# Moving the conversion of four weight tiles out of the ramp, and re-ordering loads, stores and scalings of a fused attention and FFN kernel on eight cores

## The chip, the cores and the metric

The kernel runs on all eight NeuronCores of one Trainium2 chip. Each core gets two of the sixteen batch entries and does the whole layer for them, with no traffic between cores. The metric is the device time in microseconds of the slowest core.

## The reference

```python
h = layernorm(x)                                  # x: 16 x 2048 x 1024 float32
q, k, v = h @ Mq, h @ Mk, h @ Mv                  # 8 heads, 64 wide for q and k, 128 for v
scores = einsum('bhqk,bhck->bhqc', q, k)          # q, k, v are plain reshapes to (b, h, 2048, .)
att = softmax(scores / 8, axis=1)                 # over the query axis, of each (b, h)
x = x + layernorm(att @ v)
wg, wu, wd = (w_int * (1 / 127) for w_int in (w_gate, w_up, w_down))   # int32 weights, 3072 hidden
f = (silu(h2 @ wg.T) * (h2 @ wu.T)) @ wd.T        # h2 = layernorm(x)
x = x + layernorm(f)
```

The reshape to heads takes rows of the sequence into a head: a head's 2048 positions are 256 rows of x. The softmax runs over queries, so its sums belong to the rows of V, which are scaled by their reciprocals before the second product.

## The kernel before, in words

**The ramp and the projection.** A core holds 32 tiles of 128 rows of x, in eight blocks of four tiles. `load_x(T)` loads tile T into one of four buffers `xl`, `ln1(T)` normalises it to bf16 `xn` (statistics on VectorE, the power -0.5 on GpSimd, the scaling on ScalarE, whose `finish` also issues the load of tile T+4), and `turn(T)` transposes it on TensorE into `xnT` (L282, copied out by ScalarE, for T = 2 and 3 by VectorE). `proj_units(blk, ...)` makes sixteen units of eight matmuls 128x128x512 of a block: four for q, four for k, eight for v (L327). `evac` empties their banks, VectorE and ScalarE by turns. Blocks 0 to 3 use four PSUM banks (`wide`), blocks 4 to 7 two, because the attention has started beside them. The results go to scratch in HBM: `qk_d` from `qst` and `kst`, `v_d` from `vst`, with stores on SP's queue. The float32 weights mq, mk and mv come as three loads that cast to bf16, on GpSimd's queue.

**The attention.** It is cut into 256 steps K. A step's score unit `s_unit(K)` makes four matmuls into S, one ScalarE instruction makes the exponentials with their sums (L432), `v_scale(K, c)` multiplies the left (c = 0) and the right (c = 1) half of the V tile by the reciprocal sums on VectorE (L440, L441), and `av_unit(K, c)` makes 16 matmuls 128x128x128 into banks O. A V tile's halves lie in twelve buffers `vt`: slots 0 to 5 for c = 0, 6 to 11 for c = 1. `av_unit(K, c)` issues the load of step K+6 into the slot that it has just read (`load_v`, on SP's queue). `unload` adds O to `y2`, and after sixteen steps `half_stats` and `ln2` normalise, add x (tiles that `load_x1` has loaded a second time, into `x1`) and build the bf16 `x2T` for the FFN.

**The FFN.** Eight blocks n of 512 rows. For each of 24 hidden tiles `gate_unit` and `up_unit` make eight matmuls each from `wgu` (four buffers, bf16, gate and up of one hidden tile) and `x2T`; then sixteen `down_unit` make twelve each from `hT` and `wd`. The gate and up weights are int32 in HBM, 1 MB a hidden tile. `convert(c)` is a DMA on GpSimd's queue from HBM to HBM that casts two hidden tiles to bf16 scratch `gu_bf`; twelve of them stand at fixed units of the projection (L716, L717), each behind a wait for the matmul before it. `load_wgu(i)` loads a 0.5 MB tile from that scratch, 192 times, on SP's queue; `load_wd` casts the down weights in FFN block 0.

**What sets the order.** The program is written out by a planner on the host. Every engine executes its own list, in the order in which the planner emitted it, and each DMA stands in the list of the engine that issues it (`P.dma("sync", ...)`, `"gpsimd"`, `"scalar"`). `P.tick` and `P.spent` move the planner's clock by the units' estimated times; `P.later(d, fn)` emits fn once that clock is d us further. `run_side` puts score and AV units between the main units. Per four steps the side order is: AV of steps 4Q and 4Q+1, c = 0, behind the score unit of 4Q+3; AV of 4Q+2 and 4Q+3, c = 0, behind 4Q+4; c = 1 of the first two behind 4Q+5, of the last two behind 4Q+6. The attention runs 41 steps beside blocks 4 to 7 of the projection, and 32 beside each FFN block. An engine that waits for one instruction holds all that stand behind it in its list.

## Time and profile before

| | us |
|---|---|
| median of three runs (1749.59 to 1753.48) | 1753.07 |
| profiled execution, its device time | 1755.92 |
| its span (first to last instruction, slowest core, core 1) | 1754.4 |
| spans of the eight cores | 1731.6 to 1754.4 |
| TensorE busy in the span | 1669.3 |
| VectorE, ScalarE, GpSimd busy | 951.2, 814.8, 125.5 |
| granted TensorE clock of core 1, mean | 0.983 |

Busy times are of core 1, the slowest. In the rows of the trace PE is TensorE, DVE is VectorE, ACT is ScalarE, POOL is GpSimd, SPq is SyncE's instruction queue; L76 is the helper that issues every DMA and L72 the one that issues every matmul, so such rows are told apart by tile names. A name such as `F<-wv,xnT` gives what is written and what is read, with buffer numbers left out.

### The profile page before, as it was taken

The page shows a single profiled execution, that of the slowest core. Times are in us where ns is not written, and L with a number is a line of the kernel's source. Part 1 is how long each engine was busy: PE and PEld are TensorE (multiplying, and loading weights), DVE is VectorE, ACT ScalarE, POOL GpSimd, SP SyncE. Part 2 cuts the span into 40 slices and gives each one's busy share as a digit, 9 for nine tenths or more (in the row PEclk, how much of TensorE's full clock was granted, in tenths as well). Part 3 has the DMA queues.
Part 4 walks back from the last instruction along what each step waited for, and adds up shares of the span by engine and source line. Part 5 has one row for each costly group of instructions (what it writes and reads, how often), then busy time and mean ns, then how long its engine had stood idle before and what let it go on. Part 6 is the DMA issues. An engine that isn't in the chain of part 4 may idle for free.

```text
span 1754.4 us, 32046 instructions; the slowest of 8 cores (1731.6 to 1754.4 us)
## 1 busy us (share of the span) xinstructions
PE 1669.3 (95%) x11008; PEld 795.4 (45%) x11008; DVE 951.2 (54%) x2123; ACT 814.8 (46%) x984; POOL 125.5 (7%) x257
## 2 busy tenths in 40 slices
PE   5999888879999999999999999999999999999998
PEld 2444444434444444444444444444444444444443
DVE  3433446355646565656465656575657565655433
ACT  3444556445535454455445545454455444542111
POOL 2111001000101000100010001000100010001000
PEclk9999999989999999999999999999999999999999
DMA  9899997978982656265626563666256625651531
GB/s 191 175 190 216 201 170 143 196 152 215 235 213 85 205 168 178 88 202 160 186 88 193 168 189 85 185 171 195 88 169 180 198 78 171 167 160 52 157 96 48
DMA packets 212446, 281.02 MB, mean 160 GB/s; under 512 B 48320, under 2 KB 132288, under 8 KB 212288
## 3 DMA queue, kind: packets, MB, share of 16 engines
q1 hardware_dynamic: 199568, 255.91, 51.5%
q0 software_dynamic: 12720, 23.07, 10.4%
q8 instruction: 91, 1.49, 0.4%
q14 instruction: 67, 0.55, 0.1%
HBM read 260.05 MB, written 46.14 MB: 175 GB/s over the span
## 4 chain that ended last, share of the span: by engine, by line
PE 76%; DMA 8%; DVE 7%; ACT 4%; issue 3%; SPq 1%; POOL 1%; DVEq 0%; ACTq 0%; POOLq 0%
PE F L72 55%; PE O L72 13%; PE S L72 7%; DMA vt<-v_d 5%; ACT E L432 1%; DMA xl<-x 1%; DMA wgu<-gu_bf 1%; ACT y L500 1%; DMA wq<-mq 1%; SPq L76 1%; DVE x L507 1%; DVE hT L573 1%; DVE bnB L487 0%; ACT y L251 0%; DVE y L470 0%
## 5 line engine op out<-in xcount | busy, mean ns | idle before, releaser
L72 PE MATMUL F<-x2T,wgu 128*128 128x512 bf16 x3072 | 764.5, 380 | 14.5 <-DVE rsx L440 3.9
L432 ACT ACTIVATE E<-S 128x2048 bf16<-128x2048 f32 x256 | 480.4, 1876 | 542.1 <-PE S L72 542.1
L72 PEld LDWEIGHTS F<-x2T,wgu 128*128 128x128 bf16 x3072 | 260.1, 97 | 359.4 <-issue 157.6
L72 PE MATMUL F<-wd_sb,hT 128*128 128x512 bf16 x1536 | 357.6, 379 | 0.4 <-ACT y L601 0.4
L72 PEld LDWEIGHTS O<-vt,E 128*128 128x128 bf16 x4096 | 271.0, 98 | 147.8 <-issue 37.4
L72 PE MATMUL O<-vt,E 128*128 128x128 bf16 x4096 | 313.4, 220 | 21.0 <-DVE vt L441 19.4
L550 DVE SCALAR_TENSOR_TENSOR th<-th,F 128x512 f32<-128x512 f32 x192 | 131.8, 687 | 347.9 <-ACT th L546 347.8
L441 DVE TENSOR_SCALAR vt<-vt,rsx 128x512 bf16<-128x512 bf16 x512 | 179.3, 351 | 94.8 <-DMA vt<-v_d 49.4
L72 PEld LDWEIGHTS F<-wd_sb,hT 128*128 128x128 bf16 x1536 | 141.6, 98 | 168.2 <-issue 23.6
L72 PE MATMUL S<-qk 64*128 64x512 bf16 x1024 | 158.1, 388 | 5.6 <-ACT E L432 5.3
L546 ACT ACTIVATE th<-F 128x512 f32<-128x512 f32 x192 | 113.4, 591 | 72.8 <-PE F L72 72.7
L573 DVE TENSOR_TENSOR hT<-th,F 128x512 bf16<-128x512 f32 x192 | 131.1, 683 | 19.7 <-DVE vt L441 10.2
L470 DVE TENSOR_TENSOR y<-y,O 128x512 f32<-128x512 f32 x192 | 122.8, 680 | 25.1 <-PE O L72 25.0
L72 PE MATMUL F<-wv,xnT 128*128 128x512 bf16 x384 | 95.8, 387 | 3.2 <-ACT kst L314 2.2
L72 PEld LDWEIGHTS S<-qk 64*128 64x128 bf16 x1024 | 29.5, 94 | 117.3 <-issue 117.3
L500 ACT ACTIVATE y<-y,nbB,rsB 128x512 f32<-128x512 f32 x64 | 48.6, 806 | 65.2 <-POOL nbB L247 65.2
L237 POOL TENSOR_TENSOR rsB<-vfB,mhalf 128x1 f32<-128x1 f32 x64 | 39.2, 612 | 512.5 <-DVE vfB L235 469.8
L613 POOL TENSOR_TENSOR rsC<-vfC,mhalf 128x1 f32<-128x1 f32 x31 | 20.5, 662 | 715.0 <-DVE vfC L611 715.0
L255 DVE TENSOR_TENSOR x<-x,y 128x1024 f32<-128x1024 f32 x31 | 38.0, 1224 | 58.8 <-ACT y L251 58.8
L251 ACT ACTIVATE y<-y,nbC,rsC 128x1024 f32<-128x1024 f32 x31 | 38.3, 1236 | 51.6 <-POOL nbC L247 51.6
L72 PE MATMUL F<-xnT,wk 128*128 128x512 bf16 x192 | 51.5, 409 | 10.5 <-DVE rsx L440 10.0
L251 ACT ACTIVATE xn<-xl,nbA,rsA 128x1024 bf16<-128x1024 f32 x32 | 39.7, 1240 | 44.4 <-POOL nbA L247 44.3
(75 smaller groups left out, 886.2 us busy)
## 6 DMA issues: line engine op xcount, KB each, us to landing
wgu<-gu_bf SPq DMA_DIRECT2D x192, 512.0 KB, 4.8
vt<-v_d SPq DMA_DIRECT2D x512, 128.0 KB, 3.0
xl<-x SPq DMA_DIRECT2D x32, 512.0 KB, 10.5
x<-x SPq DMA_DIRECT2D x32, 512.0 KB, 6.2
out<-x SPq DMA_DIRECT2D x31, 512.0 KB, 3.2
gu_bf<-gu POOLq DMA_DIRECT2D x12, 1024.0 KB, 18.7
v_d<-vst SPq DMA_DIRECT2D x16, 512.0 KB, 14.6
qk<-qk_d SPq DMA_DIRECT2D x16, 512.0 KB, 5.8
```

What stands on the lines that cost most here:

```text
L72: "tensor", lambda t: t.matmul(out, lhsT, rhs, start=start, stop=stop),
L237: return P.pool(lambda g: g.tensor_tensor(rs[:, s:s + 1], vf[:, s:s + 1], mhalf[:, 0:1], AL.pow), t, const_done)
L251: return P.act(lambda a: a.activation(dst[:, :], y[:, :], AF.Identity, bias=nb[:, s:s + 1], scale=rs[:, s:s + 1]), *waits)
L255: return P.dve(lambda v: v.tensor_tensor(xt[:, :], xt[:, :], y[:, :], AL.add), *waits)
L432: lambda s: s.activation(to, S[:, :], AF.Exp, scale=0.125, accum_out=accx[:, K % 16:K % 16 + 1]),
L441: vs_tok[K, c] = P.dve(lambda v: v.tensor_scalar(v_[:, :], v_[:, :], r, None, AL.mult), rs_tok[K], v_tok[K, c])
L470: t = P.dve(lambda v, d=d, part=part: v.tensor_tensor(part, part, O[d][:, :], AL.add), done, y2_tok[u, d])
L500: t = [P.act(lambda e, part=part: e.activation(part, part, AF.Identity, bias=nbB[:, s:s + 1], scale=rsB[:, s:s + 1]), shift) for part in h ...
L546: tanh = P.act(lambda s: s.activation(t_[:, :], F[0][:, :], AF.Tanh, scale=1.0 / 254.0), done, th_read[i - 1] if i else None, *(() if i el ...
L550: bank_free["F0"] = gated[i] = P.dve(lambda v: v.scalar_tensor_tensor(t_[:, :], t_[:, :], 1.0, F[0][:, :], AL.add, AL.mult), tanh)
L573: lambda v: v.tensor_tensor(dst, t_[:, :], F[1][:, :], AL.mult), done, gated[i],
L613: b = P.pool(lambda g: g.tensor_tensor(rsC[:, s:s + 1], vfC[:, s:s + 1], mhalf[:, 0:1], AL.pow), b, const_done)
```

## The change

It does these things, in the order of the program:

- Tiles 0 to 3 of x are loaded straight into `x1` and kept there; `load_x1` skips them. Tiles 4 to 7 are loaded once the first half of mk has landed. Loads of tiles 8 to 31 are issued by ScalarE.
- mk and mv come in two pieces each, mk's by rows and mv's by columns, and the two of mk are issued between the first normalisations. A one-element activation stands at the start of ScalarE's list.
- Block 0's four key units become `keys_at_once`, which goes through four banks at each of eight row slices and waits for mk's second piece at the fifth. Block 1's q and k units become sixteen `narrow_unit` of 256 columns, so that the first eight need only tiles 4 and 5. V units of blocks 0 and 1 come left halves first.
- Stores of q and k are issued by ScalarE, 1.4 us later by the planner's clock. V is stored for two blocks at once, in pieces of 512 elements in place of 256, by ScalarE for pairs 0 and 2 and by SyncE for pairs 1 and 3; `load_v` waits for the one store that it needs.
- `v_scale` is emitted later: 9.0, 9.0, 6.5, 3.6 us (c = 0) and 20.0, 15.5, 14.0, 11.0 us (c = 1) behind the step's exponential by K % 4, in place of 3.6 and 6.5; `av_unit` emits it if it has not been.
- Twenty hidden tiles are converted, one by one, ten of them from unit 22 in steps of four and ten from the tenth unit of block 4 in steps of five. Hidden tiles 0 to 3 are cast straight into `wgu` by GpSimd's queue in FFN blocks 0 and 1, and in block 1 `keep_wgu` stores them to the scratch, from which the other six blocks load them.
- `load_wgu` is emitted 1.7 us later, the down weights come in 24 loads of one tile from unit 3 on, and the second `half_stats` hangs on a place in the side order.

```diff
-SLOT = 5.1
+CAST = 4
...
     def load_x(T, *waits):
-        xl_tok[T] = P.dma("sync", xl[T % 4][:, :],
-                          x_hbm[T // 16, 128 * (T % 16):128 * (T % 16 + 1), :],
-                          q_xl[T % 4], *waits)
+        dst, q = (x1[T], q_x1[T]) if T < 4 else (xl[T % 4], q_xl[T % 4])
+        xl_tok[T] = P.dma("sync" if T < 8 else "scalar", dst[:, :],
+                          x_hbm[T // 16, 128 * (T % 16):128 * (T % 16 + 1), :], q, *waits)
+        if T < 4:
+            x1_tok[T] = xl_tok[T]
...
-        ready = ln_stats(xl[s], bnA, mvA, vfA, rsA, s, EPS, xl_tok[T])
+        src = x1[T] if T < 4 else xl[s]
+        ready = ln_stats(src, bnA, mvA, vfA, rsA, s, EPS, xl_tok[T])
...
-                load_x(T + 4, t, w_tok[0])
+            t = xl_free[T] = xn_tok[T] = ln_scale(xn[s], src, rsA, nbA, s, ready, busy)
+            if 8 <= T + 4 < 32:
+                load_x(T + 4, t)
...
-        if T in (2, 3) or T >= 20 and T % 2:
+        if T in (0, 1, 2, 3, 4, 6) or T >= 20 and T % 2:
...
+        def keys_at_once():
...
+            for dt in range(8):
+                for i, (name, ap) in enumerate(four):
+                    first = [bank_free.get(name), *ready, *w_ready[1][:1]] if dt == 0 else \
+                        w_ready[1][1:] if dt == 4 else ()
+                    tok = P.mm(ap, wk[:, 512 * dt + 128 * i:512 * dt + 128 * (i + 1)],
+                               xT[:, 512 * dt:512 * (dt + 1)], dt == 0, dt == 7, first, done=dt == 7)
+                    done.append(tok)
...
+        def narrow_unit(which, i, g):
...
+            for dt in range(8):
+                first = [bank_free.get(name), *w_ready[which],
+                         *(xnT_tok[4 * blk + 2 * g + j] for j in range(2))] if dt == 0 else ()
+                done = P.mm(ap[:, 0:256], w[:, 512 * dt + 128 * i:512 * dt + 128 * (i + 1)],
+                            xT[:, 512 * dt + 256 * g:512 * dt + 256 * (g + 1)], dt == 0, dt == 7, first,
+                            done=dt == 7)
+            P.spent(4 * MM, 0.5)
...
+        def qk_store(which, ev=None):
...
-                    "sync", bass.AP(qk_d.tensor, row, [[2048, 128], [128 * 2048, 2], [1, 1024]]),
+                    "scalar", bass.AP(qk_d.tensor, row, [[2048, 128], [128 * 2048, 2], [1, 1024]]),
...
+            P.later(1.4, store)
...
-            ready = [w_tok[2], xnT_tok[4 * blk + j]]
+            ready = [w_tok[f"v{c2}"], xnT_tok[4 * blk + j]]
...
+            st = vst[2 * (pair % 2) + half]
+            dst = bass.AP(st, 2048 * c2 + 256 * par + 128 * hh, [[4096, 128], [512, 4], [1, 128]])
+            v_ev[blk, j, c2] = bank_free[name] = evac(dst, ap, done, v_stored.get((pair - 2, half)))
+            if par and hh == 1 and c2 == 1:
...
+                def store():
+                    v_stored[pair, half] = P.dma(
+                        "scalar" if pair % 2 == 0 else "sync",
+                        bass.AP(v_d.tensor, (16 * b + half) * 131072 + 512 * (pair % 2),
+                                [[1024, 128], [2 * 131072, 8], [1, 512]]),
+                        bass.AP(st, 0, [[4096, 128], [512, 8], [1, 512]]), q_vs[2 * (pair % 2) + half], *ev)
+                if pair % 2:
+                    store()
+                else:
+                    P.later(1.4, store)
...
+        if blk == 0:
+            units[4:8] = [keys_at_once]
+        if blk == 1:
+            units[0:8] = [lambda w=w, i=i, g=g: narrow_unit(w, i, g)
+                          for g in range(2) for w in range(2) for i in range(4)]
...
-        stored = [v_stored[4 * b + 2 + p, h] for p in range(2) for h in range(2)]
         v_tok[K, c] = P.dma("sync", vt[i][:, :], v_d[16 * b + t, :, 512 * c:512 * (c + 1)], q_v[i],
-                            *stored, av_tok[K - 6, c] if K >= 6 else None)
+                            v_stored[2 * b + c, t % 2], av_tok[K - 6, c] if K >= 6 else None)
...
     def load_x1(n):
+        if n < 4:
+            return
...
-        P.later(3.6, lambda: v_scale(K, 0))
-        P.later(6.5, lambda: v_scale(K, 1))
+        P.later((9.0, 9.0, 6.5, 3.6)[K % 4], lambda: v_scale(K, 0))
+        P.later((20.0, 15.5, 14.0, 11.0)[K % 4], lambda: v_scale(K, 1))
...
     def v_scale(K, c):
+        if (K, c) in vs_tok:
+            return
...
     def av_unit(K, c):
+        v_scale(K, c)
...
-            for d in range(2):
-                P.later(1.5 + SLOT * d, lambda d=d: half_stats(G, c, d))
+            P.later(1.5, lambda: half_stats(G, c, 0))
+            if G == 1:
+                P.later(4.1, lambda: half_stats(G, c, 1))
+            else:
+                hooks[side_at[0] + 4] = lambda: P.later(1.5, lambda: half_stats(G, c, 1))
...
-        ht = i % NHT
-        wgu_tok[i] = P.dma("sync", bass.AP(wgu[i % 4], 0, [[2048, 128], [1024, 2], [1, 1024]]),
-                           gu_bf[ht, :, :, 0:1024], q_wgu[i % 4],
-                           conv_tok[ht], *([wgu_read[i - 4]] if i >= 4 else xl_idle))
+        ht, free = i % NHT, [wgu_read[i - 4], conv_tok[(i - 4) % NHT]] if i >= 4 else xl_idle
+        if i < 2 * NHT and ht < CAST:
+            wgu_tok[i] = P.dma("gpsimd", wgu[i % 4][:, :], gu_hbm[ht, :, :], q_cast[i % 4], *free)
+        else:
+            wgu_tok[i] = P.dma("sync", bass.AP(wgu[i % 4], 0, [[2048, 128], [1024, 2], [1, 1024]]),
+                               gu_bf[ht, :, :, 0:1024], q_wgu[i % 4], conv_tok[ht], *free)
+    def keep_wgu(ht):
+        conv_tok[ht] = P.dma("sync", gu_bf[ht, :, :, 0:1024],
+                             bass.AP(wgu[ht % 4], 0, [[2048, 128], [1024, 2], [1, 1024]]), q_keep[ht],
+                             wgu_tok[NHT + ht])
...
+        if n == 1 and ht < CAST:
+            keep_wgu(ht)
...
-            load_wgu(i + 4)
+            P.later(1.7, lambda: load_wgu(i + 4))
...
+            if side_at[0] in hooks:
+                hooks.pop(side_at[0])()
...
+    load_w("q", 0, wq, mq_hbm, 512, (0, 8), (0, 512), xl_tok[0])
+    ln1(0)
+    load_w("k0", 1, wk, mk_hbm, 512, (0, 4), (0, 512))
+    P.tick(1.75)
+    ln1(1)
+    load_w("k1", 2, wk, mk_hbm, 512, (4, 4), (0, 512))
+    for T in range(4, 8):
+        load_x(T, w_tok["k0"])
+    P.tick(1.75)
+    w_ready = [[w_tok["q"]], [w_tok["k0"], w_tok["k1"]]]
+    ln1(2)
+    turn(0)
...
     def convert(c, *waits):
-        conv_tok[2 * c] = conv_tok[2 * c + 1] = P.dma(
-            "gpsimd", bass.AP(gu_bf.tensor, 2 * c * 256 * ROW, [[2 * ROW, 256], [ROW, 2], [1, 1024]]),
-            bass.AP(gu_hbm.tensor, 2 * c * 262144, [[2048, 256], [1024, 2], [1, 1024]]), q_conv[c], *waits)
+        conv_tok[c] = P.dma(
+            "gpsimd", bass.AP(gu_bf.tensor, c * 256 * ROW, [[2 * ROW, 128], [ROW, 2], [1, 1024]]),
+            bass.AP(gu_hbm.tensor, c * 262144, [[2048, 128], [1024, 2], [1, 1024]]), q_conv[c], *waits)
...
-    first = u0[0:8] + u1[0:8] + u0[8:16] + u1[8:16]
+    for unit in u0[0:4]:
+        unit()
+        P.tick(4 * MM)
+    ln1(4)
+    ln1(5)
+    load_w("v0", 3, wv, mv_hbm, 1024, (0, 8), (0, 512))
+    u0[4]()
+    turn(4)
+    turn(5)
+    ln1(6)
+    ln1(7)
+    load_w("v1", 4, wv, mv_hbm, 1024, (0, 8), (512, 512))
+    for unit in u1[0:8]:
+        unit()
+    turn(6)
+    turn(7)
+    for unit in u1[8:16]:
+        unit()
+    first = u0[5::2] + u0[6::2] + u1[16::2] + u1[17::2]
...
-    early_conv = {22: 0, 32: 1, 42: 2, 52: 3}
-    later_conv = {(4, 6): 4, (4, 14): 5, (5, 6): 6, (5, 14): 7, (6, 6): 8, (6, 14): 9, (7, 4): 10, (7, 10): 11}
...
+    early_conv = {22 + 4 * c: CAST + c for c in range(10)}
+    later_conv = {(4 + u // 16, u % 16): CAST + 10 + c for c, u in enumerate(range(9, 59, 5))}
...
-            if blk == 7 and u == 4:
+            if blk == 7 and u in (3, 6, 9, 12):
                 xl_idle = [*(xl_free[T] for T in range(28, 32)), xn_read[28]]
-                for i in range(4):
-                    load_wgu(i)
+                load_wgu(u // 3 - 1)
...
     def load_wd(c, *waits):
-        src = bass.AP(wd_hbm.tensor, 2 * c * 131072, [[1024, 128], [131072, 2], [1, 1024]])
-        dst = bass.AP(wd, 2 * c * 1024, [[NHT * 1024, 128], [1024, 2], [1, 1024]])
-        wd_tok[:] = [P.dma("gpsimd", dst, src, q_wd, *ramp_idle, *waits)]
-    first_block = {}
-    for c in range(12):
-        first_block[6 + 4 * c // 3] = lambda *w, c=c: load_wd(c, *w)
+        wd_tok[:] = [P.dma("gpsimd", wd[:, 1024 * c:1024 * (c + 1)], wd_hbm[c, :, :], q_wd,
+                           *ramp_idle, *waits)]
...
-            if n == 0 and ht in first_block:
-                first_block[ht](("c_tensor", P.count["c_tensor"]))
+                if n == 0 and 3 <= 2 * ht + (unit is up_unit) <= 41:
+                    at = 2 * ht + (unit is up_unit) - 3
+                    for c in range(24 * at // 39, 24 * (at + 1) // 39):
+                        load_wd(c, ("c_tensor", P.count["c_tensor"]))
```

**Where the order changes.** VectorE's list in FFN block 1, around the scaling of the V tiles of steps 96 to 98 (vt0 to vt2 are their left halves, vt6 and vt7 the right halves of 96 and 97; bnB, bnC, y2, y4 and x1 belong to the normalisations). Before:

```order
L440 RECIPROCAL rsx<-accx 128x1
L441 TENSOR_SCALAR vt0<-vt0,rsx 128x512
L487 BN_STATS bnB<-y2_1 128x6
L441 TENSOR_SCALAR vt6<-vt6,rsx 128x512
L440 RECIPROCAL rsx<-accx 128x1
L441 TENSOR_SCALAR vt1<-vt1,rsx 128x512
L487 BN_STATS bnB<-y2_1 128x6
L608 BN_STATS bnC<-y4_0 128x6
L441 TENSOR_SCALAR vt7<-vt7,rsx 128x512
L440 RECIPROCAL rsx<-accx 128x1
L441 TENSOR_SCALAR vt2<-vt2,rsx 128x512
```

In the change the same stretch of VectorE's list, a piece of eight rows left out:

```order
L508 RECIPROCAL rsx<-accx 128x1
L509 TENSOR_SCALAR vt0<-vt0,rsx 128x512
L559 BN_STATS bnB<-y2_1 128x6
L692 BN_STATS bnC<-y4_0 128x6
L508 RECIPROCAL rsx<-accx 128x1
L509 TENSOR_SCALAR vt1<-vt1,rsx 128x512
...
L508 RECIPROCAL rsx<-accx 128x1
L509 TENSOR_SCALAR vt2<-vt2,rsx 128x512
L509 TENSOR_SCALAR vt6<-vt6,rsx 128x512
L509 TENSOR_SCALAR vt7<-vt7,rsx 128x512
```

The right halves (vt6, vt7) moved from right behind their left halves to behind step 98's left half.

GpSimd's list at the start. Before, the loads of mk and mv stand behind the four normalisations of block 0:

```order
L76 DMA wq<-mq 128x8x512
L237 TENSOR_TENSOR rsA<-vfA,mhalf 128x1
L247 TENSOR_SCALAR nbA<-mvA,rsA 128x1
...
L76 DMA wk<-mk 128x8x512
L76 DMA wv<-mv 128x8x1024
```

In the change:

```order
L76 DMA wq<-mq 128x8x512
L244 TENSOR_TENSOR rsA<-vfA,mhalf 128x1
L254 TENSOR_SCALAR nbA<-mvA,rsA 128x1
L76 DMA wk<-mk 128x4x512
L244 TENSOR_TENSOR rsA<-vfA,mhalf 128x1
L254 TENSOR_SCALAR nbA<-mvA,rsA 128x1
L76 DMA wk<-mk 128x4x512
...
L76 DMA wv<-mv 128x8x512
```

The first half of mk moved up past three normalisations, the second past two.

SyncE's list from the end of the first four projection blocks. Before, stores of q, k and v and loads of x stand among the V loads:

```order
L76 DMA v_d<-vst 128x8x256 x2
L76 DMA qk<-qk_d 128x2048
L76 DMA qk<-qk_d 64x1024 x2
L76 DMA vt<-v_d 128x512 x12
L76 DMA xl<-x 128x1024 x2
L76 DMA qk_d<-qst 128x2x1024
L76 DMA xl<-x 128x1024
```

In the change:

```order
L76 DMA v_d<-vst 128x8x512 x2
L76 DMA qk<-qk_d 128x2048
L76 DMA qk<-qk_d 64x1024 x2
L76 DMA vt<-v_d 128x512 x12
L76 DMA qk<-qk_d 128x2048
L76 DMA qk<-qk_d 64x1024 x2
L76 DMA vt<-v_d 128x512 x26
```

The loads of x and the stores of q and k have left this list; they now stand in ScalarE's, between its copies.

## Rows read from the trace of the kernel before

**Rows 1.** Core 1 by stretches: length, busy PE, PEld, DVE, ACT, POOL, PEclk, DMA share, GB/s.

```profile
0.00:62.90 62.90, 39.91 (x193) 18.90 (x194) 23.45 (x53) 21.70 (x23) 11.39 (x28) 0.95 0.89 192
62.90:160.00 97.10, 97.10 (x528) 47.09 (x526) 38.32 (x79) 42.70 (x52) 13.52 (x31) 1.00 0.97 186
160.00:200.00 40.00, 35.69 (x264) 17.20 (x262) 16.16 (x43) 26.79 (x31) 3.03 (x7) 1.00 1.05 212
200.00:400.00 200.00, 166.04 (x1199) 81.78 (x1196) 99.12 (x244) 103.87 (x122) 16.92 (x32) 0.89 0.84 170
400.00:560.00 160.00, 153.62 (x1056) 73.34 (x1054) 93.80 (x212) 77.80 (x96) 17.60 (x30) 0.99 0.79 194
560.00:737.70 177.70, 175.74 (x1218) 84.20 (x1216) 106.05 (x240) 89.30 (x109) 9.86 (x20) 1.00 0.54 158
```

**Rows 2.** Timeline of the ramp: start us, us, engine line op [idle before <-releaser].

```profile
13.13 0.69 DVE L229 BATCH_NORM_STATS2 bnA<-xl 128x6 f32<-128x512 f32 x1
...
18.50 1.93 PE L292 MATMUL tp<-ident,xn 128*128 128x128 bf16 x16 [4.31 <-ACT xnT L300]
...
21.37 3.57 PE L72 MATMUL O<-xnT,wq 128*128 128x512 bf16 x8 [0.94 <-DVE xnT L298]
...
34.33 3.27 PE L72 MATMUL O<-xnT,wk 128*128 128x512 bf16 x8 [3.17 <-DMA wk<-mk]
...
47.29 3.50 PE L72 MATMUL O<-xnT,wq 128*128 128x512 bf16 x8 [1.25 <-ACT xnT L300]
...
62.79 1.89 PE L72 MATMUL O<-wv,xnT 128*128 128x512 bf16 x8
64.51 1.67 PE L72 MATMUL F<-wv,xnT 128*128 128x512 bf16 x7
```

**Rows 3.** DMA queues (packets, MB, share of 16 engines) and issues (median us to landing).

```profile
q1 hardware_dynamic: 199568, 255.91, 51.5%
q0 software_dynamic: 12720, 23.07, 10.4%
...
wv<-mv POOLq DMA_DIRECT2D x1, 2048.0 KB, 38.9
```

**Rows 4.** Waits from 160 to 560 us: total, times, longest.

```profile
DVE vt L441 <- DMA vt<-v_d: 49.4, 13, 10.9
...
PE O L72 <- DVE vt L441: 19.4, 5, 8.8
...
PE F L72 <- DVE rsx L440: 10.9, 4, 6.6
```

**Rows 5.** Timeline around 210 us.

```profile
210.60 0.35 DVE L441 TENSOR_SCALAR vt<-vt,rsx 128x512 bf16<-128x512 bf16 x1 [5.97 <-DMA vt<-v_d]
...
214.74 0.68 DVE L313 CAST kst<-F 128x512 bf16<-128x512 f32 x1
...
215.56 1.87 PE L72 MATMUL F<-xnT,wk 128*128 128x512 bf16 x4 [6.63 <-DVE rsx L440]
```

**Rows 6.** The chain of waits from 160 to 520 us: start us, us, what.

```profile
189.27 21.24 DMA vt<-v_d
...
231.98 15.06 DMA vt<-v_d
...
312.10 15.81 DMA vt<-v_d
...
334.96 19.33 DMA vt<-v_d
...
486.07 18.53 DMA wgu<-gu_bf
```

**Rows 7.** SyncE's queue from 90 to 137 us.

```profile
102.06 8.85 SPq L76 DMA_DIRECT2D xl<-x  x1
...
134.73 9.99 SPq L76 DMA_DIRECT2D qk_d<-qst  x1
```

**Rows 8.** Waits from 560 to 1600 us.

```profile
PE F L72 <- DVE rsx L440: 3.5, 12, 0.4
```

More of the change, by code:

```diff
@@ L145, in build @@
     q_xl = [P.sem(f"q_xl{i}") for i in range(4)]
[L146 removed]
+    q_w = [P.sem(f"q_w{i}") for i in range(5)]
     q_qks = [P.sem(f"q_qks{i}") for i in range(NBLK)]
@@ L350, in qk_unit @@
             if i == 3:
-                ev = [qk_ev[n] for n in range(4)]
-                row = 2 * blk * 128 * 2048 + 1024 * which
+                qk_store(which)
+        def keys_at_once():
+            ready = [xnT_tok[4 * blk + j] for j in range(4)]
+            four, done = [next_bank(banks) for i in range(4)], []
+            for dt in range(8):
[6 more added lines that the diff above has]
+                P.spent(4 * MM, 0.5)
+            for i, (name, ap) in enumerate(four):
+                dst = bass.AP(kst[par], 256 * i, [[2048, 128], [1024, 2], [1, 256]])
+                qk_ev[i] = bank_free[name] = evac(dst, ap, done[28 + i])
+            qk_store(1)
@@ new lines, in narrow_unit @@
+        def narrow_unit(which, i, g):
+            w, st = (wq, qst[par]) if which == 0 else (wk, kst[par])
+            name, ap = next_bank(banks)
+            for dt in range(8):
[4 more added lines that the diff above has]
+                            done=dt == 7)
+            P.spent(4 * MM, 0.5)
+            qk_ev[g, i] = bank_free[name] = evac(
+                st[:, 1024 * g + 256 * i:1024 * g + 256 * (i + 1)], ap[:, 0:256], done)
+            if g and i == 3:
+                qk_store(which, [qk_ev[a, n] for a in range(2) for n in range(4)])
@@ L693, in build, with load_w @@
[L693 to L701 removed]
+    def load_w(name, q, w, src, cols, rows, part, *waits):
+        lo, n = rows
+        at, width = part
+        w_tok[name] = P.dma(
+            "gpsimd", bass.AP(w, lo * cols + at, [[8 * cols, 128], [cols, n], [1, width]]),
+            bass.AP(src.tensor, 128 * lo * cols + at, [[cols, 128], [128 * cols, n], [1, width]]),
+            q_w[q], *waits)
```

73 lines of the change are left out of this document (32 added, 41 removed).

## The prediction

> **What bounds the kernel now.** I read the busy times by stretches first. The reader is to see three regimes of TensorE [rows 1]. In the ramp (0 to 62.9 us) it is busy 39.9 us. In the first four projection blocks (62.9 to 160) it is never idle, though the DMA share is 0.97. From 160 to 400 us it is idle 4.3 + 34.0 = 38.3 us, and its clock is granted at 0.89 of full from 200 on, which with the two levels 2.4 and 1.2 GHz means up to 22% of these 200 us at the lower one and up to 22 us lost by it (less, since some of it falls on idle time). From 400 to 560 it is idle 6.4 us, and from then on it is as good as full: 2.0 us idle in 177.7, where no wait for a V load is listed any more and TensorE's for VectorE's reciprocals are 3.5 us in a thousand [rows 1, 8]. So of 1754 us only the first 560 have anything to give, some 23 + 38 + 6 us of idle and the slow clock, and nothing that speeds up VectorE, ScalarE or the transfers later on is worth a microsecond.
>
> Then the waits of that stretch, for who ends it. VectorE waits 49.4 us for V tiles, TensorE 19.4 us for the scaled V tiles and 10.9 us for VectorE's reciprocals [rows 4]. The timeline shows what the last is: the scaling of a V tile stands in VectorE's list, its load has not landed, the copy of a key bank stands behind it, and TensorE, which wants that bank, waits 6.63 us [rows 5]. It is a wait passed on by the order of VectorE's list, not by its load. The chain has four such loads of 15.1 to 21.2 us from issue to landing, and one load of gate and up weights of 18.5 us [rows 6].
>
> **The change part by part.** *The ramp.* Queries of block 0 start at 21.37, keys at 34.33 after a wait of 3.17 for mk, block 1 at 47.29 and V at 62.79 [rows 2]. Now: the statistics of tile 3 start at 13.13 as before, its transposes no longer wait for ScalarE's copies of tiles 0 and 1 (the 4.31 us), so I put the first query matmul at 19.5, about 1.9 earlier. Queries take 34.33 - 3.17 - 21.37 = 9.8 us as before, clock start included, to 29.3 [rows 2]. The keys need no wait if mk lands by then; it landed at 34.3, and now its halves are issued behind the first and the second normalisation in place of the fourth, and no longer with the whole of mv right behind. 32 matmuls at the pitch of V's (a unit of eight takes 64.51 - 62.79 = 1.72 us [rows 2]) are 6.9 us, to 36.2. Four transposed tiles cost 1.0 each at the slow clock (16 matmuls, 1.93 us [rows 2]); I take 2.4 for the four at full clock. Block 1's eight units' worth of columns is 13.8. That is 52.4. V begins 10.4 us earlier. Ends: 4 us if block 1's tiles or mk come late, since the same 8 MB of float weights must come (mv lands 38.9 us after its issue, rows 3, at 56 us); 12 if nothing waits. I take 10.4, since mv's right half is needed only at 52.4 + 6.9 = 59.3. The warm-up activation costs nothing, it stands where ScalarE is idle.
>
> *Bytes.* Over the whole span the queue of casting transfers took 10.4% of the engines for 23.07 MB, 7.9 us a MB landed; the other 51.5% for 255.91 MB, 3.5 us a MB [rows 3]. A hidden tile is 0.52 MB: 4.1 us to cast, 1.85 to load. Before the FFN the four cast tiles save a load each, 4 x 1.85 = 7.4 us, and the four kept tiles of x 7.4 more: 14.8 us of the DMA's time. The wider pieces of V may save some of the 29 us that its 8.4 MB of stores cost at 3.5 us a MB; I count none of it. In FFN block 1 the casts cost 4 x (4.1 - 1.85) and the stores to scratch 4 x 1.85, 16.4 us of DMA; the DMA share is 0.54 there, 82 us are free, and the tiles are fetched four hidden tiles ahead, some 20 us. It costs nothing. Without that cover it would be a wait for a load like the one of 18.5 us [rows 6], 4 us each beyond what is fetched ahead, 16 in all.
>
> *The projection beside attention.* A right half of step 4Q+6 is loaded behind the AV of step 4Q, one place before its own score unit, and was scaled 6.5 us after that. At the FFN's pace a place is 177.7 / 32 = 5.6 us [rows 1]: 12.1 us of lead. Now it is 5.6 + 14.0 = 19.6. Of the four loads of the chain three are inside 19.6, the fourth is 1.6 us beyond [rows 6]. So of the 19.4 + 10.9 = 30.3 us that TensorE waits for scalings [rows 4] about 80%, 24 us, have their cause removed, and a share of the slow clock with them, some 12 us by the same ratio. Against it: the DMA is busy 1.05 x 40 + 0.84 x 200 = 210 of these 240 us [rows 1], 195 with the bytes saved, and a shorter stretch packs them closer. I take 28 us (20 of idle, 8 of clock), which puts the share at 195 / 212 = 0.92, a share at which the stretch before it runs without a stall [rows 1]. Ends: 8 (only the list's order helps, each late load still ends a wait in TensorE) and 48 (all idle above the later rate, 38.3 - 2.6, and 12 of clock).
>
> *Stores and x loads on ScalarE.* ScalarE is idle for a third to a half of the stretch [rows 1], and an issue on a free queue is short. But SyncE's queue shows issues of 8.9 and 10.0 us in the first four blocks [rows 7], and an issue held that long on ScalarE holds copies. Taken as zero here, a rival below. *FFN block 0:* idle above the later rate is 6.4 - 1.8 = 4.6, and 1.6 of clock; the down weights spread over 98 us in place of 75, so I take 4 (ends 0 and 6). *Everything after:* the scalings of 4Q+1 now stand 9.0 us behind an exponential whose AV follows two places, 10.0 us, later, a margin of 1.0; those of 4Q+3 had 5.0 - 3.6 = 1.4 and gave next to none [rows 8]. Zero, with a rival.
>
> Sum: 10.4 + 28 + 4 = 42.4. The profiled execution took 1755.92, 1.5 more than its span and 2.85 over the median of 1753.07. 1755.9 - 42.4 = 1713.5; against the median 1710.7. I predict 1712.
>
> **The rivals.** *A shared DMA that gives nothing back.* The V loads now share SyncE's list with little else. The rows say only that V loads in a list with stores took 15 to 21 us [rows 6]; whether it waited behind them or beside them they don't say. If beside, landings stay at 15 to 21 us, the earlier start of V packs the same bytes into less time, and the stretch gives 12 in place of 28, the ramp 4: 1755.9 - 4 - 12 - 2 = 1738, 1736 by the median. The Trainium skill, "DMA: Bandwidth & Descriptors", section "Issuing engines are not separate DMA queues", says just this: transfers run on the same 16 engines whoever issues them, and only issue time is saved. Its section "Queues, rings and completion order" says each engine goes round the queues packet by packet, by which a V load would overtake stores of another queue. No run here shows either. Chance 0.18.
>
> *ScalarE held by its own stores.* Two pairs of V stores and the stores around them now stand there. At 9 us each [rows 7], less the 3.4 us that two free banks of 1.72 cover, four are worth some 4 x 5.5 = 22: 1712 + 22 = 1734. Against it speaks that TensorE never idled there [rows 1], so the DMA has room for its work. Chance 0.10.
>
> *Slower: scalings too late.* If the planner's 1.0 us of margin is not there on the chip, the left halves of every fourth step reach TensorE late, in all 64 groups of four. Late by d, that costs 64 x d, and from d = 0.66 us it eats all of the 42. At d = 1 it is 64 us: 1776. The row that speaks against it is the margin of 1.4 us that gave no wait. Chance 0.05.
>
> *More than I take.* All of the middle's 48, 12 in the ramp and 6 in block 0: 1755.9 - 66 = 1690. It needs a DMA share near 1.0 without waits, as from 62.9 to 160. Chance 0.10.
>
> **How the numbers follow.** My forecast, 1700 to 1726, has 0.57. The range takes in the upper part of the better case, all of the held ScalarE and the shared DMA: 1696 to 1740. A measurement of this kernel can tell about 0.2%, 3.5 us. Slower needs the late scalings, or ScalarE's holds together with a shared DMA: 0.05. Within 0.2%: 0.02. Faster: 0.93.
>
> **What would show it.** V's first matmul at 52 us, not 62.8. The row "DVE vt <- DMA" from 160 to 560 down from 49.4 to some 10, and TensorE's waits for scalings from 30 to some 6. Clock of the 200 us before the FFN above 0.94. V loads of 20 us still there, but not in the chain. FFN blocks from the third on 177 us each, as now. Wrong I am if an FFN block takes more than 178.5, if ScalarE shows DMA issues of several us with TensorE waiting behind its copies, or if V starts at 52 and the FFN still starts where it did.

## The result and the profile after

The changed kernel takes 1756.64 us and the kernel before, beside it, 1749.61: medians of 17 executions each, with the three of twenty in which the cores of a die ran at a lower clock left out here and in every median below (with them 1758.78 and 1750.43). The ratio of their times is 1.004, with a 95% interval of 1.0026 to 1.0055: slower by 0.4%, where I had forecast 1712 and had given 0.05 to slower. The profiled execution spans 1755.1 us on core 7, the slowest; the eight cores lie between 1733.4 and 1755.1.

To see where it went I take five moments from the traces, by TensorE's matmuls: the first that reads `wv` (V), the first that writes `S` (scores), the first gate matmul (FFN), and the first gate matmul of FFN block 1, then of block 7. Each is the median of the eight cores, in us from the span's start.

| | V | scores | FFN | block 1 | block 7 | end |
|---|---|---|---|---|---|---|
| before | 62.4 | 161.5 | 371.3 | 554.5 | 1608.2 | 1742.9 |
| after | 54.5 | 167.6 | 364.7 | 552.1 | 1611.8 | 1746.9 |
| the stretch that ends there, after - before | -7.9 | +14.0 | -12.7 | +4.2 | +6.0 | +0.4 |

The last row adds up to +4.0 for the median cores of these two executions; over all runs the slowest core loses some 7 us. These moments are of one execution of each kernel, so the table shows where to look, and the runs below decide. By it two gains came, and three losses that I had priced at nothing, or as a gain, took them back. FFN block 0 (+4.2) is the least certain: taken core by core it lasts 181.0 to 187.6 us before and 180.0 to 193.6 after, medians 184.5 and 187.0.

By stretches, core 7, the columns of [rows 1]:

```profile
0.00:54.50 54.50, 36.68 (x257) 24.13 (x258) 23.09 (x52) 18.45 (x24) 11.80 (x27) 1.00 0.95 199
54.50:171.20 116.70, 98.88 (x532) 47.27 (x531) 43.63 (x91) 46.17 (x55) 19.05 (x42) 0.95 0.97 199
171.20:367.00 195.80, 173.93 (x1331) 87.38 (x1332) 104.25 (x261) 120.62 (x140) 23.35 (x42) 0.98 0.75 155
367.00:560.00 193.00, 176.54 (x1215) 84.29 (x1213) 102.18 (x236) 88.66 (x107) 25.57 (x46) 0.97 0.80 185
711.00:889.90 178.90, 175.40 (x1218) 84.31 (x1216) 104.89 (x241) 89.75 (x109) 11.26 (x20) 1.00 0.53 157
```

The ramp ends 8 us sooner. The first projections, never idle before, are idle 116.7 - 98.9 = 17.8 us, and their clock is 0.95 in place of 1.00. Beside attention the clock is 0.98 on this core and the DMA share is down to 0.75, and TensorE is nevertheless idle 21.9 us. (Over the eight cores, from first scores to FFN, the median clock rose from 0.94 to 0.97, and two cores stayed at 0.94.) FFN block 0 is idle 16.5 us on this core, and a later block takes 178.9 us in place of 177.7.

**Ahead of the first scores.** The chain of waits of core 7:

```profile
96.14 5.20 ACTq L76
...
148.52 11.86 SPq L76
...
162.02 9.07 DMA qk<-qk_d
```

And SyncE's queue in the timeline, which shows what stood ahead:

```profile
144.59 3.83 SPq L76 DMA_DIRECT2D v_d<-vst  x2
148.52 14.07 SPq L76 DMA_DIRECT2D qk<-qk_d  x3
```

The first load of queries and keys is issued behind two V stores of 1 MB each. It is three DMAs: the issue of the first alone takes 11.86 us, the last then lands 9.07 us after its own issue, and TensorE waits. The waits from 160 to 560 us, core 7, answer to [rows 4]:

```profile
PE S L72 <- DMA qk<-qk_d: 13.3, 1, 13.3
...
PE F L72 <- DMA wgu<-gu_bf: 11.7, 2, 9.0
...
PE O L72 <- DVE vt L509: 5.6, 5, 2.0
PE O L72 <- DVE rsx L508: 4.8, 4, 2.2
```

VectorE's waits for V loads, 49.4 us before, have no row any more. Two others stand out: 13.3 us for the first Q/K load, on other cores 4.4 to 14.5, where it was at most 1.1 before, and 11.7 for gate and up tiles, on other cores 0 to 8.2, where it was 2.2 to 7.2 before.

**Beside attention** the rows for `O` are my step in reverse. The timeline of core 0:

```profile
254.93 0.16 DVE L508 RECIPROCAL rsx<-accx 128x1 f32<-128x1 f32 x1
...
255.27 0.35 DVE L509 TENSOR_SCALAR vt<-vt,rsx 128x512 bf16<-128x512 bf16 x1 [0.18 <-DVE rsx L508]
...
255.77 0.70 PE L72 MATMUL O<-vt,E 128*128 128x128 bf16 x8 [2.15 <-DVE rsx L508]
```

No load is late. TensorE has arrived at the AV product, and the scaling is only now made. Nine AV groups on this core wait so (the two rows for `O` read the same here), up to 2.2 us each and 10.4 in all.

**In a later FFN block** (core 7, timeline):

```profile
709.21 0.69 DVE L236 BATCH_NORM_STATS2 bnB<-x 128x6 f32<-128x512 f32 x1
...
709.62 1.52 ACT L572 ACTIVATE y<-y,nbB,rsB 128x512 f32<-128x512 f32 x2 [5.06 <-POOL nbB L254]
...
711.05 1.85 ACT L498 ACTIVATE E<-S 128x2048 bf16<-128x2048 f32 x1
...
713.14 0.61 PE L72 MATMUL S<-qk 64*128 64x512 bf16 x4 [1.71 <-ACT E L498]
```

ScalarE has waited 5.06 us for the norm of one half before it scales `y`; the exponential stands behind that, and TensorE waits 1.71 us for the bank of scores. The waits from 560 to 1600 us put numbers on it, core 7:

```profile
PE S L72 <- ACT E L498: 8.5, 5, 1.7
PE F L72 <- DVE hT L657: 8.3, 6, 1.4
```

Before, core 1, the second had no row of that size (its place was held by [rows 8]), and the first was:

```profile
PE S L72 <- ACT E L432: 4.5, 5, 1.3
```

### The profile page after: what moved, and what is told of

It is laid out like the page before. It is cut to its first block, busy times and chain, and to the rows that moved or that the text cites. A ratio compares the mean times of both kernels' runs of the same rounds, so it can differ in the third digit from the quotient of the medians.

```text
span 1755.1 us, 32318 instructions; the slowest of 8 cores (1733.4 to 1755.1 us)
## 1 busy us (share of the span) xinstructions
PE 1654.7 (94%) x11072; PEld 798.0 (45%) x11072; DVE 945.8 (54%) x2131; ACT 815.7 (46%) x985; POOL 150.8 (9%) x287
## 4 chain that ended last, share of the span: by engine, by line
PE 73%; DVE 9%; DMA 5%; issue 5%; ACT 4%; SPq 1%; ACTq 1%; POOL 1%; DVEq 0%; POOLq 0%
PE F L72 54%; PE O L72 12%; PE S L72 6%; DMA wgu<-gu_bf 2%; ACT E L498 1%; DMA wv<-mv 1%; DVE y L539 1%; DVE x L579 1%; DVE bnB L559 1%; ACT y L572 1%; DVE hT L657 1%; SPq L76 1%; DVE th L634 1%; ACTq L76 1%; DMA wq<-mq 1%
## 5 line engine op out<-in xcount | busy, mean ns | idle before, releaser
L72 PE MATMUL F<-x2T,wgu 128*128 128x512 bf16 x3072 | 763.3, 380 | 28.6 <-DMA wgu<-gu_bf 11.7
L509 DVE TENSOR_SCALAR vt<-vt,rsx 128x512 bf16<-128x512 bf16 x512 | 166.5, 350 | 46.8 <-DVE rsx L508 46.7
L72 PE MATMUL S<-qk 64*128 64x512 bf16 x1024 | 155.9, 383 | 23.5 <-DMA qk<-qk_d 13.3
L244 POOL TENSOR_TENSOR rsB<-vfB,mhalf 128x1 f32<-128x1 f32 x64 | 43.2, 674 | 480.3 <-DVE vfB L242 446.4
L692 DVE BATCH_NORM_STATS2 bnC<-y 128x6 f32<-128x512 f32 x62 | 42.8, 691 | 37.2 <-ACT y L685 35.4
L72 PE MATMUL F<-xnT,wk 128*128 128x512 bf16 (+1 forms) x208 | 50.3, 377 | 4.1 <-DVE kst L325 3.3
## 6 DMA issues: line engine op xcount, KB each, us to landing
gu_bf<-gu POOLq DMA_DIRECT2D x20, 512.0 KB, 10.4
```

Source lines behind the costliest of these rows:

```text
L72: "tensor", lambda t: t.matmul(out, lhsT, rhs, start=start, stop=stop),
L244: return P.pool(lambda g: g.tensor_tensor(rs[:, s:s + 1], vf[:, s:s + 1], mhalf[:, 0:1], AL.pow), t, const_done)
L509: vs_tok[K, c] = P.dve(lambda v: v.tensor_scalar(v_[:, :], v_[:, :], r, None, AL.mult), rs_tok[K], v_tok[K, c])
L692: b = P.dve(lambda v: v.bn_stats(bnC[:, o:o + 6], y[:, lo:lo + 512]), t)
```

## The experiments

Each is judged against runs of the kernel before on the same chip. The expectations were written before the runs. In the diffs the lines with - are the changed kernel's.

### One part undone at a time

**The half statistics** (`half_stats`) at their old distances:

```diff
-            P.later(1.5, lambda: half_stats(G, c, 0))
-            if G == 1:
-                P.later(4.1, lambda: half_stats(G, c, 1))
-            else:
-                hooks[side_at[0] + 4] = lambda: P.later(1.5, lambda: half_stats(G, c, 1))
+            for d in range(2):
+                P.later(1.5 + 5.1 * d, lambda d=d: half_stats(G, c, d))
```

> The change with the second half of the attention's statistics emitted as before (5.1 us behind the first by the planner's clock) in place of four side places later. In the changed kernel FFN blocks from the second on take 178.6 to 179.2 us in place of 177.5 (core 7 against core 1), with TensorE waiting 1.87 us for an exponential in each down phase where it waited 0.96, and 1.53 us for hT once a block, where it waited for nothing. Theory A (the moved statistics do this, through VectorE's and GpSimd's lists to the scaling of y that stands ahead of the exponential on ScalarE): the blocks are back at 177.5, and the kernel is 6 to 7 us faster than the change, near 1752. Theory B (the later scalings of V do it): the blocks stay at 178.7 and the time does not move.

Measured: 1742.51 us, ratio to before 0.9948 (0.9925 to 0.9972). Theory A was right. FFN blocks 1 to 5 are back at 177.3 from 178.8. Its waits from 560 to 1600 us, core 7:

```profile
PE S L72 <- ACT E L498: 4.0, 5, 0.8
PE F L72 <- DVE th L631: 2.5, 10, 0.5
```

Both rows of the changed kernel are gone or halved. FFN start came 6.1 us earlier as well and block 0 8.0 shorter by the medians of the moments, which I had not expected; both stretches have such statistics too. Core by core block 0 is only 4.0 shorter in the median, and lasts from 177.3 to 192.2 us.

**The V scalings** at 3.6 and 6.5 us:

```diff
-        P.later((9.0, 9.0, 6.5, 3.6)[K % 4], lambda: v_scale(K, 0))
-        P.later((20.0, 15.5, 14.0, 11.0)[K % 4], lambda: v_scale(K, 1))
+        P.later(3.6, lambda: v_scale(K, 0))
+        P.later(6.5, lambda: v_scale(K, 1))
```

> The change with V scaled 3.6 and 6.5 us behind each exponential, as before. Theory B: FFN blocks back at 177.5. Theory A: they stay at 178.7. My prediction's reason, that the late scalings free VectorE's list beside the projection: the stretch from the first score matmul to the first gate matmul grows again, from 197 towards the 210 us of before (medians of the cores), and the kernel is up to 13 us slower than the change. The rival, that V loads now land in 2 to 5 us because the stores and the loads of x have left SyncE's queue: scalings wait for nothing even at 3.6 and 6.5 us, the stretch stays within 3 us of 197.

Measured: 1745.27 us, ratio 0.9952 (0.9936 to 0.9968). The FFN blocks stay at 178.3 or more, so they are not the scalings' doing. But from the first scores to the FFN it took 185.0 us in place of 197.1, 12 us less, where one theory had it up to 13 us longer and its rival the same. TensorE's waits there, core 0, 160 to 380 us:

```profile
PE S L72 <- DMA qk<-qk_d: 9.4, 1, 9.4
...
PE O L72 <- DVE vt L509: 0.8, 1, 0.8
```

The late scalings did not help this kernel: they cost it 12 us, in the very stretch in which I had counted on them.

**The first Q/K load** ahead of the last two V stores:

```diff
+        if u == 58:
+            load_qk(0)
         unit()
...
-    load_qk(0)
     for K in range(6):
```

> The change with the first load of q and k for the scores issued six units earlier, ahead of the two V stores of a megabyte each on SyncE's queue. In the changed kernel its issue takes 11.86 us behind them and TensorE stands 13.5 us before the first scores. Theory C (the place behind the big stores costs it): the first scores come 10 to 13 us earlier and the FFN starts 7 to 13 us earlier; near 1747. Rival D (the DMA is short of time in this stretch and takes it back at the first V tiles, or further on): the first scores come earlier but the FFN starts within 3 us of where it did.

Measured: 1749.98 us, ratio 0.9994 (0.9973 to 1.0014). Scores begin at 160.8 in place of 167.6, the FFN at 355.3 in place of 364.7. The wait for the load is gone on all eight cores. But on cores 1, 5 and 7 scores still begin at 171.8, 165.5 and 169.9, and there the issues on ScalarE's queue show up. Core 1, timeline and waits:

```profile
101.20 11.42 ACTq L76 DMA_DIRECT2D xl<-x  x1
```

```profile
PE O L72 <- ACT qst L326: 6.0, 1, 6.0
```

An issue of 11.42 us holds ScalarE, and TensorE waits 6.0 us for the copy behind it.

**No cast tiles**, all 24 converted:

```diff
-CAST = 4
+CAST = 0
...
-    later_conv = {(4 + u // 16, u % 16): CAST + 10 + c for c, u in enumerate(range(9, 59, 5))}
+    later_conv = {(4 + u // 16, u % 16): CAST + 10 + c for c, u in enumerate(range(6, 62, 4))}
```

> The change with all 24 hidden tiles converted through HBM (ten early, fourteen in blocks 4 to 7, steps of four units) and loaded from there in every block: the casts into the buffers and the store in block 1 undone. Theory E (the casts of block 1, issued while block 0 still loads its last tiles, make the load of 23.8 us and the 9.1 us that TensorE waits before tile 23): FFN block 0 gets shorter from 187.4 towards 183 (medians), and block 1 is unchanged; before the FFN the four more conversions cost up to 7 us. Net near the change, 1752 to 1760. Rival F (the wait comes from the loads of x, q and k alone, issued at the same time): block 0 stays at 187.

Measured: 1748.55 us, ratio 0.9975 (0.9958 to 0.9992). Block 0 takes 181.6 us in place of 187.4, and TensorE's waits for `wgu<-gu_bf` are 0 to 3.3 us on the eight cores, in place of 0 to 11.7.

### The two causes I had named, each alone

**All loads and stores back on SyncE** (x loads, q/k stores, the V stores of even pairs: `"sync"` for `"scalar"`), nothing else.

> The changed kernel with x loads, q/k stores and the V stores of pairs 0 and 2 back on SP's queue; nothing else. Theory C (the queues set it): V loads, which landed in 2 to 5 us with the stores on ScalarE's queue and in 15 to 21 before, go back to over 10 us, VectorE waits for vt again, and S to FFN start is 8 us longer than 197; on the other hand ScalarE's issue stalls of 5 us before S go. Total 1763 to 1768. Rival C2 (the fewer descriptors of V stores in pairs did it, 16 in place of 32, not the queue): V loads stay at 2 to 5 us and the time is 1755 to 1758.

Measured: 1747.73 us, ratio 0.9982 (0.9959 to 1.0006). Both theories fall on the time: by the ratios it is 10 us faster than the change, not slower. Scores begin at 160.5 in place of 167.6 (the first Q/K load costs 5.4 to 8.2 us on the eight cores, not 4.4 to 14.5), the FFN at 355.6; from scores to FFN it is 195.1 us, 2 less than with two queues. FFN block 0 on the other hand takes 193.4 in place of 187.4 in this execution, with waits for `wgu<-gu_bf` of 2.2 to 12.0 us on seven cores; that was not taken apart. And the landing of V loads, the median between first scores and FFN on core 0 (last number, us), before, after, and with everything on SyncE:

```profile
vt<-v_d SPq DMA_DIRECT2D x73, 128.0 KB, 9.4
```

```profile
vt<-v_d SPq DMA_DIRECT2D x76, 128.0 KB, 4.4
```

```profile
vt<-v_d SPq DMA_DIRECT2D x75, 128.0 KB, 5.6
```

So 3.8 of the 5.0 us by which V loads became shorter don't need a queue of their own. The same median on the eight cores, from 165 to 355 us, is 7.9 to 9.8 before, 3.8 to 5.1 after, and 5.4 to 7.0 with everything on SyncE: the queue has a share, the smaller one. The DMA moved less in that stretch, in fewer packets. Before, then after, core 0:

```profile
DMA packets 31444, 37.99 MB, mean 184 GB/s; under 512 B 5151, under 2 KB 21952, under 8 KB 31424
```

```profile
DMA packets 24735, 30.00 MB, mean 150 GB/s; under 512 B 6044, under 2 KB 18443, under 8 KB 24715
```

**The late scalings alone, in the kernel before** (the two `P.later` lines as in the change, and a scaling made at once if its product comes first).

> The kernel before with the late V scalings alone (9.0, 9.0, 6.5, 3.6 and 20.0, 15.5, 14.0, 11.0 us after the exponential, and a scaling made at once where the product would come first). My prediction's step said that scalings waiting for slow V loads hold VectorE's list, and that making them late frees it. By that theory S to FFN start falls from 209.8 us to about 195 and the time to 1738. Rival: the scalings are late for their own products, whatever the loads do, as the changed kernel with early scalings showed (12 us faster there): S to FFN start stays or grows by up to 12 us, and the time is 1751 to 1763, the FFN blocks unchanged at 177.5.

Measured: 1741.95 us, ratio 0.9948 (0.9928 to 0.9968). From scores to FFN 202.3 us in place of 209.8. There my theory held in its sign and in half its size: where V loads are slow, late scalings free VectorE's list, and they gave 7.5 us of the 15 that I had expected. VectorE's waits for V loads from 160 to 360 us fell on core 0 from

```profile
DVE vt L441 <- DMA vt<-v_d: 43.5, 7, 14.5
```

to

```profile
DVE vt L443 <- DMA vt<-v_d: 20.7, 5, 16.2
```

What stayed is one gap of 15.30 us in TensorE. Core 0, TensorE, then SyncE's queue ahead of it:

```profile
351.11 1.01 PE L72 MATMUL O<-vt,E 128*128 128x128 bf16 x8 [15.30 <-DVE vt L443]
```

```profile
321.80 7.27 SPq L76 DMA_DIRECT2D wgu<-gu_bf  x4
329.16 2.92 SPq L76 DMA_DIRECT2D vt<-v_d  x4
332.34 3.26 SPq L76 DMA_DIRECT2D qk_d<-kst  x1
335.70 12.45 SPq L76 DMA_DIRECT2D vt<-v_d  x6
```

The first four gate and up tiles, 2 MB, and a store of keys stand just ahead of V loads for which TensorE waits; which of the two holds them was not tried. In the changed kernel those four tiles come as casts on GpSimd's queue.

### The parts undone together

**Three undone**: half statistics, scalings, first Q/K load.

> Three parts of the change undone at once: the second-norm statistics (half_stats) at their earlier distances, the two V scalings at 3.6 and 6.5 us after the exponential as before, and the first Q/K load issued ahead of the last two V stores on SP. If each part cost what it did alone (after 1758.8; the three alone 12.6, 13.5 and 7.3 us below it, by medians) and they cost in different places, the sum is 33 us: 1725 us, FFN blocks 177.4, S begins at 160.5, FFN starts near 345. Rival: the 12 us that the scalings at 3.6 and 6.5 gave in the projection stage and the 9 us that the earlier Q/K load gave at FFN start are the same slack; then FFN starts near 351 and the time is 1732.

Measured: 1730.41 us (three executions), ratio 0.9867 (0.9833 to 0.9901). FFN at 351.2, later blocks 177.2. The rival was right: scalings and Q/K load share their slack.

**Three undone and no casts**:

> The one before it, and no gate and up tile cast from the integers: all 24 converted, in both first FFN blocks, as before. With the casts alone away the time fell by 9.8 us, 5.8 of them in FFN block 0 and 2.9 ahead of it. If the wait in block 0 for tile 23 is the cast loads' doing, block 0 goes from about 181 to 179 here and the whole is 3 to 9 us below the run with the casts: 1717 to 1722. Rival: the converts of 24 tiles on ScalarE and GpSimd cost as much elsewhere (FFN starts later by 3 us): no difference.

Measured: 1724.51 us (three executions), ratio 0.9841 (0.9819 to 0.9864): 5.9 us below the run beside it, 4.6 by the ratios, whose intervals overlap.

**Four undone**: half statistics, scalings, casts, and everything on SyncE.

> The changed kernel with four parts undone: second-norm statistics and V scalings at their earlier distances, no cast tiles, and x loads, q/k stores and all V stores on SP's queue (with V stores still in pairs, the split weight loads and the new start). The run without the casts (1724.6) had the stores on ScalarE; with them on SP the changed kernel was 10.6 us faster, 7.1 of it ahead of S, 2 between S and the FFN start. Since the first Q/K load stood early in that run, most of the 7.1 is had already (S began at 161.2): 1717 to 1723. Rival: early scalings need V loads that land soon, and with the stores on one queue they land in 5 to 11 us instead of 2 to 5: waits of VectorE for vt come back, S to FFN start is over 190, and the time is 1728 or more.

Measured: 1722.46 us, ratio 0.9849 (0.9828 to 0.9871): by the ratios 1.9% below the change and 1.5% below the kernel before, the fastest, in a tie with the one above and the one below. From scores to FFN 189.0 us.

**And the first Q/K load early**:

> The same with the first Q/K load ahead of the last two V stores. S began at 160.5 with the stores on SP without it, and the earliest the last K projection allows is about 158: a gain of 0 to 3 us over the run beside it. Rival: one store less ahead of it delays the V stores and with them the V loads: 0 to 4 us slower.

Measured: 1723.72 us, ratio 0.986 (0.9834 to 0.9886). Scores begin at 154.3 in place of 160.8, where I had held 158 to be the earliest possible, but the FFN at 348.9 in place of 349.8: on one queue the 6.5 us are lost again before the FFN. This run closes the account of the 14.0 us ahead of the scores. From V's first matmul to the scores, medians:

| us | Q/K load behind the V stores | ahead of them |
|---|---|---|
| x loads, q/k and V stores partly on ScalarE's queue | 113.1 | 105.9 |
| all on SyncE's | 105.9 | 100.8 |

The kernel before takes 99.1. The queue and the order gave 7.2 us each when undone alone and 12.3 together; the other parts undone in this run act only behind the first scores.

**Four undone but the casts**:

> The first of these with the four cast tiles of FFN blocks 0 and 1 kept. The casts cost 9.8 us in the changed kernel, and 8.8 with three parts undone; if the wait for tile 23 in block 0 is theirs, it is there again: block 0 181 in place of 179, FFN start 3 us later, the whole 5 to 9 us over the run without casts. Rival: what they cost was the collision with ScalarE's queue of x loads and stores, which is empty now: within 2 us.

Measured: 1732.47 us, ratio 0.9905 (0.988 to 0.9929), 10.0 us over the run without casts, and not by a constant: block 0 takes 178.7, 183.3, 179.1, 186.1, 178.9, 183.0, 180.6 and 192.2 us on cores 0 to 7, where it takes 178.7 to 180.2 without. The median core loses 1 us, the slowest sets the time. Core 7, SyncE's queue, then the casts' issues:

```profile
451.08 1.05 SPq L76 DMA_DIRECT2D x<-x  x2
453.38 1.64 SPq L76 DMA_DIRECT2D vt<-v_d  x2
455.56 0.53 SPq L76 DMA_DIRECT2D wgu<-gu_bf  x1
458.43 11.74 SPq L76 DMA_DIRECT2D vt<-v_d  x6
```

```profile
461.60 0.54 POOL L76 DMA_DIRECT2D wgu<-gu  x1
466.19 0.53 POOL L76 DMA_DIRECT2D wgu<-gu  x1 [4.06 <-PE F L72]
471.25 0.53 POOL L76 DMA_DIRECT2D wgu<-gu  x1 [4.53 <-PE F L72]
```

And the piece of the chain, and who waited:

```profile
455.56 26.43 DMA wgu<-gu_bf
```

```profile
482.24 1.86 PE L72 MATMUL F<-x2T,wgu 128*128 128x512 bf16 x4 [11.59 <-DMA wgu<-gu_bf]
```

The load of the last tile of block 0, issued at 455.56, landed at 481.99, with three casts of block 1's tiles issued behind it and read beside it.

**Casts in block 0 alone**, all 24 tiles converted:

```diff
-        if i < 2 * NHT and ht < CAST:
+        if i < 4:
```

> All 24 tiles converted, but FFN block 0's first four tiles cast straight from the integers as in the change (the fastest kernel so far with that alone added; block 1 loads them from the scratch copy). If the wait in block 0 is the work of the cast loads and copies of block 1, as its place says (loads issued at 461.6 to 471.3 us beside SP loads that took up to 26.4 us), block 0 takes 178.7 to 181 us on every core as without casts, where it took 179 to 192 with both, and the time is 1720 to 1726. Rival: the casts of block 0 shift the converts and the later loads as a whole: block 0 is spread by core again, slowest over 184, and the time is over 1728.

Measured: 1728.82 us, ratio 0.9886 (0.9856 to 0.9916), 6.5 us over the fastest by the ratios. Block 0 takes 177.4 to 180.2 us on every core: its spread was the work of block 1's casts. But the time is as the rival said, by another way: the FFN starts at 355.4, 5.6 us later, and on core 1, where it starts last, TensorE waited 14.0 us for a V tile, 23 us ahead of it:

```profile
PE O L72 <- DVE vt L509: 18.7, 3, 14.0
```

Block 0's casts are requested among the last V loads of the projection. Those casts alone don't explain it: the run before had the same four there, but only twenty tiles to convert, its FFN began at 349.2, and no core waited more than 0.7 us for a V tile in the last 25 us ahead of it (3.5 to 14.0 here). It is the casts on top of all 24 conversions.

## Why the prediction was wrong

**The ramp: right.** I took 10.4 us (ends 4 and 12); V began 7.9 us earlier. On core 7 the queries start at 19.1 (I had put 19.5) and the keys end at 35.4 (36.2); what I left out are two waits of 1.25 us for copies of transposed tiles.

**"Stores and x loads on ScalarE ... Taken as zero": wrong, by 14 us.** Two causes, by the table of the two: each undone alone gives 7.2 us, both 12.3. The first I had as a rival, a ScalarE held by its own issues: there are such issues (4.92 and 5.20 us on core 7, up to 6.67 on the eight cores), with 0 to 5.9 us of waits of TensorE for the copies behind them, and 8.1 on one core of the run with the early Q/K load; and with two queues the first Q/K load's wait is longer and more spread. The second I had not looked for: the paired V stores are of 1 MB in place of 0.5, and the last two stand on SyncE directly ahead of the first Q/K load. I had priced each issue on its own engine and never asked what is queued behind the last one.

**"The projection beside attention", 28 us: 12.7 came, and for another reason.** My step rested on the lead of late scalings over slow loads. In the kernel before that is true and worth 7.5 us. In the changed kernel it cost 12, and the rest of the change gave 24.8 (185.0 without the late scalings, 209.8 before): V loads land in 4.4 us there, nothing is late, and the scalings are made at or behind the time their product is due. The step took the loads of 15 to 21 us [rows 6] as given while the same change took 8 MB out of the stretch. The two parts don't add: each cures the same wait, and the second has only its price left. The clock came back above the 0.94 that I had named (0.98 on core 7, 0.97 in the median), but not on every core. That 12.7 lies so near the 12 of the rival of a shared DMA is luck: its reason was that landings stay at 15 to 21 us, and they didn't. As for "a shared DMA that gives nothing back": the Trainium skill, "DMA: Bandwidth & Descriptors", section "Issuing engines are not separate DMA queues", says that another issuing engine saves issue time alone. The landings of 4.4 and 5.6 us, with 9.4 before, agree with it in the main, though the second queue did make them some 1.2 us shorter; the issue time was not saved here, it moved to ScalarE.

**"FFN block 0 ... I take 4": wrong sign, +4.2; and "It costs nothing" of block 1's casts.** The term used the DMA share of block 1, 0.54. Tiles are fetched four ahead, so these casts are issued at the end of block 0, where the share is 0.80, and beside the loads of that block's last tiles, whose lateness nothing hides. I had written the price of a late load next to it (18.5 us [rows 6]) and not counted it. Measured together with block 0's casts: 11 us by the ratios in the change, 4.6 (not clear of the noise) and 10.0 in the faster versions. That block 1's casts make block 0 long and uneven is shown by the run with casts in block 0 alone: 177.4 to 180.2 us on every core. The Trainium skill, "DMA: Bandwidth & Descriptors", section "Queues, rings and completion order", says that each DMA engine goes round the queues packet by packet; the load that took 26.4 us while casts issued later were served beside it agrees with that, though no run here isolates it.

**"Everything after: zero": wrong, +6.0.** I priced the scalings there and they cost nothing: without them the blocks stay at 178.3 or more. The slower rival was right about its mechanism, scalings too late for their product, but not about the place: not in all 64 groups, but in nine groups beside the projection, the stretch in which I had counted them as a gain. The moved half statistics, which the prediction does not mention, cost 1.5 us a block (178.8 with them, 177.3 without). I had read their lines in the diff as a rewriting of the same distances. The sign I had set for myself, an FFN block over 178.5 us, is what showed it.

The terms against the median core: ramp -7.9 for -10.4, first projections +14.0 for 0, middle -12.7 for -28, block 0 +4.2 for -4, later +6.4 for 0.

**Not settled.** What gave the 24.8 us beside attention: neither the queue nor the casts (195.1 and 195.0 us without them), but paired V stores, a V load that waits for one store, kept x tiles and single conversions were not undone one by one, so that fewer bytes made V loads short is argued only. Why FFN start and block 0 shorten too with the old half statistics (6 and 8 us, where their waits explain some 1.5 a block) was not taken apart; one execution each and a block 0 that differs by core leave it open whether all of that is theirs. Nor was it taken apart why the waits for gate and up tiles in block 0 grew with everything on SyncE. Why the first Q/K load's wait is spread from 4.4 to 14.5 us with two queues and from 5.4 to 8.2 with one is only argued to be the stores and x loads of ScalarE's queue beside it.

## What to carry to other kernels

Price a prefetch in the stage in which it is issued, not in the one in which it is used, and beside the loads there whose lateness nothing hides. A change that makes loads faster and one that makes room for slow loads don't add: undo each on its own before keeping both, since the second may only cost. And list every moved instruction before summing: five things in this change, each undone alone, gave back 8 to 16 us by the ratios (statistics, scalings, casts, the queue, the order ahead of the first Q/K load), and two gains hid them.

## What the hardware did that I had not expected

An issue on SyncE, 0.3 to 0.5 us on a free queue, took 11.86 us behind two stores of 1 MB, longer than the 9.07 us that the last of its three DMAs then needed to land. Long issues I had read before [rows 7]; that a load for which TensorE waits could stand behind one I had not. On a computing engine such an issue holds the work too: 11.42 us on ScalarE, 6.0 of them passed on to TensorE. A load issued before a cast on GpSimd's queue landed after it: the one issued at 455.56 landed 26.4 us later, at 481.99, while the cast issued at 461.60 took 12.3 us and had landed at 473.9. And waits that come from such meetings differ by core, in block 0 from 178.7 to 192.2 us on cores that run the same program, so that the slowest core pays in full what the median one hardly sees.
